# Score products interleaved with the second feed-forward product, and half of the query masks ahead of the activations

## The reference, cut to what matters

```python
def favor(x, omega):
    xs = x * dh ** (-0.25)
    u = jnp.einsum('bshd,dm->bshm', xs, omega)
    h = 0.5 * jnp.sum(xs * xs, axis=-1, keepdims=True)
    return jnp.concatenate([jnp.exp(u - h), jnp.exp(-u - h)], axis=-1) * m ** (-0.5)
# causal linear attention, per head: S += k v^T, z += k; out = (q S) / (q z + eps)
for l in range(3):
    q, k, v = (out @ W[l] + b[l] for each of q, k, v)        # in heads
    a = causal_linear_attention(favor(q), favor(k), v) @ Wo[l] + bo[l]
    h = layer_norm(out + a, ln1_g[l], ln1_b[l])
    y = jax.nn.relu(h @ W1[l] + bf1[l]) @ W2[l] + bf2[l]
    out = layer_norm(h + y, ln2_g[l], ln2_b[l])
```

## Time and profile before

| | |
|---|---|
| runs | 2047.53 us (2046.19 to 2049.01) |
| the profiled execution's own time | 2053.53 us |
| its span | 2051.6 us |
| busy in the span | PE 82%, DVE 76%, POOL 48%, ACT 43% |
| `attention()` | about 632 us to 1860 us of the span |
| in 655 to 1890 us | PE 1141.79 us busy of 1235, DVE 985.58, ACT 529.05, POOL 436.63 |

### The profile page before, as it was taken

The page is one execution under the profiler, slowest core; times in us unless marked ns, Lnnn a source line. Parts: engine busy times, 40 slices in busy tenths (PEclk is TensorE's granted clock), DMA queues, the critical chain, the costliest instruction groups (busy, mean ns, idle before and its releaser), DMA issues. The chain is left out here.

```text
span 2051.6 us, 69397 instructions
## 1 busy us (share of the span) xinstructions
PE 1680.2 (82%) x28443; PEld 1259.8 (61%) x28445; DVE 1554.3 (76%) x3835; ACT 883.3 (43%) x1642; POOL 983.6 (48%) x1045
## 2 busy tenths in 40 slices
PE   5655555469937999999999989999989999995798
PEld 4332334359935666766666766666766666663798
DVE  2899965359976878878888878888868878885675
ACT  2555555446623444444444434444434444442321
POOL 0677747769953224234234224224224224223797
PEclk7877765579977999999999999999999999997899
DMA  7400011122230000000000000000000000000001
GB/s 202 86 0 0 0 24 34 34 63 63 64 111 2 3 3 3 3 3 3 3 3 3 3 4 3 3 3 3 3 4 3 3 3 3 3 3 1 16 31 37
DMA packets 60732, 42.92 MB, mean 21 GB/s; under 512 B 19720, under 2 KB 54800, under 8 KB 59952
## 3 DMA queue, kind: packets, MB, share of 16 engines
q1 hardware_dynamic: 47504, 25.35, 4.7%
q0 software_dynamic: 4352, 8.99, 1.3%
q10 hardware_dynamic: 8608, 4.67, 0.9%
HBM read 24.22 MB, written 14.77 MB: 19 GB/s over the span
## 5 line engine op out<-in xcount | busy, mean ns | idle before, releaser
L368 POOL TENSOR_TENSOR at_rstd<-at_mv,const 128x4 f32<-128x4 f32 x96 | 19.5, 203 | 570.0 <-DVE at_mv L362 569.9
L1622 PE MATMUL psum<-attn_w,at_qa 128*128 128x128 f32 x1536 | 184.1, 278 | 0.0
L1614 PE MATMUL psum<-at_vT,attn_w 128*128 128x512 f32 x384 | 180.5, 613 | 1.4 <-ACT at_vT L1427 0.9
L1622 PEld LDWEIGHTS psum<-attn_w,at_qa 128*128 128x128 f32 x1536 | 175.2, 192 | 2.7 <-issue 0.6
L1431 ACT ACTIVATE at_qa<-psum,attn_bf 128x512 f32<-128x512 f32 x192 | 132.0, 687 | 90.2 <-PE psum L1614 90.2
L1326 DVE TENSOR_SCALAR at_kb<-at_kf,const 128x512 f32<-128x512 f32 x192 | 157.9, 882 | 0.0
L1332 DVE STREAM_TRANSPOSE at_vb<-at_vT 32x512 uint32<-32x512 uint32 x192 | 134.7, 702 | 1.9
L1848 PE MATMUL psum<-tilesT,ti_masked 128*128 128x128 f32 x1024 | 119.9, 279 | 12.9 <-POOL ti_masked L1810 12.9
L1848 PEld LDWEIGHTS psum<-tilesT,ti_masked 128*128 128x128 f32 x1024 | 117.8, 195 | 14.6 <-issue 14.6
L1556 PE MATMUL psum<-at_state,at_qa 64*64 64x36 f32 x3072 | 116.8, 242 | 9.6 <-issue 9.2
L1435 ACT ACTIVATE at_qa<-at_qf,const 128x512 f32<-128x512 f32 x192 | 122.3, 710 | 0.0
(11 more groups left out here) (303 smaller groups left out, 4315.2 us busy)
## 6 DMA issues: line engine op xcount, KB each, us to landing
ex_xs<-sorted_x SPq DMA_DIRECT2D x80, 65.0 KB
x<-in_L_attn_x ACTq DMA_DIRECT2D x8, 512.0 KB, 8.5
ex_feats<-token_y SPq DMA_DIRECT2D x4, 1024.0 KB, 8.1
out<-x SPq DMA_DIRECT2D x16, 256.0 KB, 2.3
expert_w<-in_L_ffn_w SPq DMA_DIRECT2D x1, 2048.0 KB, 9.5
attn_w<-in_L_attn_W SPq DMA_DIRECT2D x2, 768.0 KB
token_y<-ex_y,ex_place POOLq DMA_INDIRECT x72
sorted_x<-ex_spare SPq DMA_DIRECT2D x1, 1040.0 KB, 8.3
```

The costliest lines, as they stand in the source:

```text
L1614: mm(bank(f.s, c), k.w1[:, f.l, c * P:(c + 1) * P], hT[f.s][:], start=True, stop=True).then_inc(hid_ready, 1)
L1622: last = mm(bank(f.s, 1)[:, c * D:(c + 1) * D], hidden[f.s][:, t, c * P:(c + 1) * P], k.w2[:, f.l, t, :], start=(t == 0 and c == 0), stop= ...
```

## The change

TensorE does the second feed-forward product in two halves and puts the first half of the scores between them; the second half of the scores stands behind the second half of the product. VectorE takes `causal(0)` ahead of the residual of `f` and `causal(1)` directly behind the statistics, ahead of all normalising; the statistics of a new group's input move behind the scan of the state. ScalarE makes the first two query masks ahead of the four activations, and the other two behind them.

```diff
 VectorE
                         last.then_inc(vb_ready, 1)
-                        if then and f and f.l == L - 1:
-                            mod_statistics(then)
                         dve.wait_ge(begun, n + 1)
                         dve.wait_ge(sum_ready, n + 1)
...
                         nc.vector.tensor_tensor_scan(...).then_inc(state_ready, 1)
+                        if then and f and f.l == L - 1:
+                            mod_statistics(then)
+                    if a:
+                        causal(0)
                     if f:
                         dve.wait_ge(ff_ready, n + 1)
                         (residual L1351, statistics)
                     if a:
-                        causal(0)
+                        causal(1)
                     ends = f and f.l == L - 1
                     if ends and then:
                         mod_normalise(then)
                     if f and not ends:
                         dve.wait_ge(res_rstd, f.count * 2 + 2)
                         normalise(... xn[f.s]).then_inc(xn_ready, 1)
-                    if a:
-                        causal(1)
 ScalarE
+                    if a:
+                        act.wait_ge(qf_ready, n + 1)
+                        masked_queries(s, 0)
                     if f:
                         for t in range(FT):  (L1431)
                     if a:
-                        act.wait_ge(qf_ready, n + 1)
-                        for i in range(HQ):  (L1435)
-                        last.then_inc(qa_ready, 1)
+                        masked_queries(s, 1).then_inc(qa_ready, 1)
 TensorE
+                def feed_forward_out(f, half):
+                    for t in (2 * half, 2 * half + 1):
+                        pe.wait_ge(hid_taken, f.count * FT + (t + 1 if t != 0 else 2))
+                        for c in range(GC):
+                            last = mm(bank(f.s, 1)[:, c * D:(c + 1) * D], hidden[f.s][:, t, c * P:(c + 1) * P], k.w2[:, f.l, t, :], ...)
+                    if half:
+                        last.then_inc(ff_ready, 1)
...
                     if f:
-                        for t in range(FT):  (L1622)
-                        last.then_inc(ff_ready, 1)
+                        feed_forward_out(f, 0)
                     if a:
                         (waits for cols_scaled, sum_taken, kb_ready, qa_ready)
                         scores(s, n, 0)
+                    if f:
+                        feed_forward_out(f, 1)
+                    if a:
                         scores(s, n, 1)
```

More of the change, by code:

```diff
@@ L1344, in slot @@
                         nc.vector.tensor_tensor_scan(whole, resets[:].rearrange("p w j -> p (w j)"), whole, 0.0, ALU.mult, ALU.add).then_inc(state_ready, 1)
-                    if f:
-                        s, n = f.s, f.count
-                        dve.wait_ge(hres_ready, n + 1)
-                        dve.wait_ge(ff_ready, n + 1)
-                        st.done(nc.vector.tensor_tensor(flat(res[s][:]), bank(s, 1), flat(hres[s][:]), ALU.add))
-                        statistics(nc, lambda c: res[s][:, c, :], stats[s], mv[s]).then_inc(res_stats, 1)
+                        if then and f and f.l == L - 1:
+                            mod_statistics(then)
                     def causal(i):
@@ L1360, in slot @@
                         causal(0)
+                    if f:
+                        s, n = f.s, f.count
+                        dve.wait_ge(hres_ready, n + 1)
+                        dve.wait_ge(ff_ready, n + 1)
+                        st.done(nc.vector.tensor_tensor(flat(res[s][:]), bank(s, 1), flat(hres[s][:]), ALU.add))
+                        statistics(nc, lambda c: res[s][:, c, :], stats[s], mv[s]).then_inc(res_stats, 1)
+                    if a:
+                        causal(1)
                     ends = f and f.l == L - 1
@@ L1401, in _, with masked_queries @@
             def _(act):
+                def masked_queries(s, half):
+                    for i in (2 * half, 2 * half + 1):
+                        last = nc.scalar.activation(qa[s][:, :, i, :], qf[s][:].rearrange("p (j i) -> p j i", i=SUB), ACT.Copy,
+                                                    scale=cst(k, "mask_a")[:, i:i + 1])
+                    return last
                 def slot(a, f, then):
@@ L1432, in slot @@
                     if a:
-                        act.wait_ge(qf_ready, n + 1)
-                        for i in range(HQ):
-                            last = nc.scalar.activation(qa[s][:, :, i, :], qf[s][:].rearrange("p (j i) -> p j i", i=SUB), ACT.Copy,
-                                                        scale=cst(k, "mask_a")[:, i:i + 1])
-                        last.then_inc(qa_ready, 1)
+                        masked_queries(s, 1).then_inc(qa_ready, 1)
                         act.wait_ge(state_ready, n + 1)
@@ L1572, in output_weights @@
                         last.then_inc(wo_ready, 1)
+                def feed_forward_out(f, half):
+                    for t in (2 * half, 2 * half + 1):
+                        pe.wait_ge(hid_taken, f.count * FT + (t + 1 if t != 0 else 2))
+                        for c in range(GC):
+                            last = mm(bank(f.s, 1)[:, c * D:(c + 1) * D], hidden[f.s][:, t, c * P:(c + 1) * P], k.w2[:, f.l, t, :],
+                                      start=(t == 0 and c == 0), stop=(t == FT - 1), skip_group_check=True)
+                    if half:
+                        last.then_inc(ff_ready, 1)
                 def slot(a, f, then):
@@ L1618, in slot @@
                     if f:
-                        for t in range(FT):
-                            pe.wait_ge(hid_taken, f.count * FT + (t + 1 if t != 0 else 2))
-                            for c in range(GC):
-                                last = mm(bank(f.s, 1)[:, c * D:(c + 1) * D], hidden[f.s][:, t, c * P:(c + 1) * P], k.w2[:, f.l, t, :],
-                                          start=(t == 0 and c == 0), stop=(t == FT - 1), skip_group_check=True)
-                        last.then_inc(ff_ready, 1)
+                        feed_forward_out(f, 0)
                     if a:
```

## The result

| | before | after |
|---|---|---|
| median of 5 runs each, us | 2047.53 (2045.37 to 2053.09) | 2056.16 (2055.66 to 2057.95) |
| ratio after to before | | 1.004, 95% interval 1.0025 to 1.0054 |
| profiled execution's own time, span, us | 2053.53, 2051.6 | 2056.23, 2054.3 |

The changed kernel is slower, by 8.6 us, and 2054 us with a range of 2042 to 2066 was predicted. The two profiled executions stand only 2.7 us apart, since that of before is 6.0 us above its own median and that of after 0.1 us.

The account below looks back on a forecast made before the run. TensorE's list was taken to set the pace, busy 1141.79 of 1235 us. To the 2047.5 us median it added 5.5 us (46 slots at 0.12) and 1 for stalls left, 6.5 more: 2054 us, range 2042 to 2066.

Parts of the forecast that it names:

- The two chains: At the slot's tail, TensorE's order and VectorE's `at_xn` chain are nearly even; the change delays `at_xn`, TensorE waits 0.9 us.
- The slot within a group: Ordinary slot forecast at 25.22 us, 0.64 more than the slot read and 0.14 less than the mean.
- the price of splitting: TensorE's feed-forward product in halves: 0.21 us for tiling changes at both ends, bounds -0.05 and 0.4.
- The stalls: TensorE's unnamed waits in small matmuls, 26.1 us before L1563, read as instruction fetch; mostly gone, 1 us left.
- The start of a group: Slot starting a new group, second such slot and the one behind: 24.82, 26.22 and 26.16 us, with GpSimd late.
- The rival by which GpSimd's lateness doesn't reach the end: Behind a new group, GpSimd's lateness doesn't reach the slot's end: 25.09 us a slot, 2036 us; chance 0.12.
- Cost nothing: ScalarE's two early masks, 1.28 us, fit its 1.32 us wait for L1614; at most 0.1 us if L1431 starts late.
- The sum: Six slots take 152.9 us, 25.48 each against 25.36; 46 slots give 5.5 us, stalls left 1, together 6.5.
- The two loop jumps: TensorE at the loop's jumps: 6.3 us lost at each, 12.6 taken out for the mean slot.
- changes of tiling are free: Rival: TensorE's tiling changes cost nothing, L1622 ends 0.96 us later, slot within a group 25.01, total 2048 us; chance 0.2.
- the stalls stay: Rival: TensorE's unnamed waits remain, each slot takes 0.64 us more, 29 us in all, 2077 us; chance 0.08.

Follow-up runs that it names:

- e8: Changed kernel with `at_xn` announced and transposed in quarters into two banks, ScalarE scaling in two halves within a group; 2046.24 us, 1.0002 of before.
- e4: Changed kernel with the second weighed half ahead of the transposes of the next input; 2068.44 us, ratio 1.0127 to before.
- e6: Kernel before with only two query masks moved ahead of ScalarE's four activations, run again on another chip; 2038.32 us, ratio 0.9959 to before.
- e9: e6's kernel with TensorE's wait for the state moved ahead of the scores, in slots within a group; 2058.26 us, ratio 1.005 to before.
- e1: Kernel before with only two query masks moved ahead of ScalarE's four activations, first look; 2037.66 us, ratio 0.9972 to before.
- e7: The changed kernel unchanged, repeated on the chip of e5, e6 and e8; 2056.24 us, ratio 1.005 to before.
- e2: Changed kernel with all four query masks back behind ScalarE's activations; 2084.86 us, ratio 1.0204 to before.
- e5: Kernel before, built anew without change and run against itself; 2048.27 us, ratio 1.0002.

## Why the prediction was right, and where it was not

**The two chains.** Right, and shown. The transposes wait 0.82 us for `at_xn` where 0.9 was said, the wait stands in 45 slots, and e8, which shortens that chain by 0.54 us, makes the slots within a group 0.34 us shorter in the mean and 0.54 at best. L1359 starts 1367.89 - 1348.73 = 19.16 us into the slot, 19.05 was said.

**The slot within a group.** 25.31 against 25.22. The slot of the earlier trace rows from which it was counted isn't a clean one: it holds an unnamed wait of 0.28 us in the first weighed half, and the shortest slots of before take 24.33. This didn't reach the forecast, which goes through VectorE's chain. The 0.09 is in the price of splitting: both halves of L1583 and of L1552 take 1.99 + 1.09 + 1.98 + 0.98 = 6.04 us from start to start, where the earlier trace rows have 875.35 - 869.66 = 5.69. One more change to the 64x64 tiling and one back cost 0.35 us, and 0.21 was taken from bounds of -0.05 and 0.4. The halves of the product came as said, 1.99 each; what was left out is that the first half of the scores takes 1.09 and not 0.96. The Trainium skill (TensorEngine Tiling (Array Packing), Key Properties) says that changing the tiling mode drains TensorE, and gives no price. These rows fit it and give a price; that it is a drain they don't show.

**The stalls.** Right on after, with more to it than was said. The unnamed waits before scores, carried state and weighed values, 39.5 us in before, are 2.6 in after. But e4 and e8 show that the wait for `at_xn` hides a part of them, and that they return when it goes. The Trainium skill (Runtime: NRT & Kernel Launch, Instruction fetch mechanics) calls the crossing of a block mostly hidden. By number the trace of before agrees: the instruction queue moved 193 packets between the starts of the second and the last slot, against 57 unnamed waits at these three places. But these cost 39.5 us, and e6 and e9 show that they move with the waits ahead of them and that kernels with the same work differ by 0.9% with them (0.9959 and 1.005, each to before on its own chip).

**The start of a group.** The parts were off, their sum not. Predicted were 24.82, 26.22 and 26.16, together 77.20; measured 25.16, 26.02 and 26.03, together 77.21. In the first slot the step from the transposes to the next slot takes 1.77 us and not 1.53, with 0.35 us of waiting for ScalarE in it where other slots have 0.17, which I had not seen, and GpSimd's L368 came 6.24 us into the slot and not 6.51. Six slots take 3 x 25.31 + 77.21 = 153.1 us, 152.9 was said. The rival by which GpSimd's lateness doesn't reach the end (2036) is out: of the 2.34 us counted, (26.02 - 25.16) + (26.03 - 25.31) = 1.58 arrive, and it needed less than 0.7.

**"Cost nothing", on ScalarE's masks.** This is the step that fell short. In the changed order the masks cost nothing, as after's timeline shows (the second pair ends at 1362.66 + 1.32 = 1363.98, the first scores start at 1364.64). But they were never weighed in the old order. Alone, in the old order, the masks gain 5 to 9 us (e1, e6), and I had said in e1's expectation that nothing would change. The profile had no row that named it: I asked only whether the array waits for the masks, and by e6 and e9 what they held up is TensorE's taking up of instructions. On the chip of e6 and e7 the change is thus 9 us won by the masks and 18 lost by the rest, and I had only the sum of the two in view. The shares hold for this order of the steps alone: in the interleaved order the same masks are worth some 29 us (e2).

**The sum.** Predicted 5.5 + 1 on the median, 6.5; measured 8.6 in medians. The traces take it apart. From the second slot's start to the last's, after takes 1183.65 - 1179.23 = 4.4 us more. The two loop jumps, which I had carried over at 12.6 us, cost 10.8 in after: 3.49 + 2.20 us for the one at 1218.61 and 3.52 + 1.56 for the other. (In before the second stands still for 3.88 us and not 3.73, so both are 12.7.) Without the jumps the slots take 6.2 to 6.3 us more, 6.5 was said, and the mean slot is 25.50 us, 25.48 was said.

The rest is the execution on which the sum rests, 6.0 us above its median. In e5 the same kernel took 2049.03, 4.5 less: 2.3 of these lie in the 46 slots, and 1.9 behind the last slot's start, which lies 219.7 us before the end in that execution and 217.8 in e5 and in after. A comparison with such an execution makes the change look cheaper than it is, by 5.9 us here; the jumps and the stretch behind the last slot take back 1.8 and 1.9. That 6.5 came as near to 8.6 as it did is therefore in part luck; that the slots were forecast to 0.1 us is not.

One sum of the prediction doesn't come out: four fifths of 0.55, 0.08 and half of 0.05 are 0.545 for slower by more, not 0.56.

**The rival "changes of tiling are free" (2048)** is out by the 0.35 us: the second half of the product ends 18.98 us into the slot, 1.28 later than in the earlier trace rows, where 1.17 was said and the rival has 0.96. So is "the stalls stay" (2077), by the waits.

What stays open: how the 23.7 us of stalls that after lost against e6 divide into those that the large matmuls between really avoid and those that only fall into the wait for `at_xn`. e4 puts 16.9 us back, but it also makes one run of 128 small matmuls out of two.

## What to carry to other kernels

When an engine's idle time has no name and lies on a grid of instructions, look at what the instruction stream waits for, not only at what the array waits for: a semaphore that is met before the array comes may still be late. Breaking up a run of small instructions helps only if what is put between doesn't feed the chain that ends the stage; here half of the scores went ahead of the one product that the next slot's input hangs on, and the steadier slot is a longer one. Take the parts of a change apart before judging it: here a part thought free was a gain and the named part the loss, and a part's worth depended on what was already in place.

## What the runs showed of the hardware

- **Fetches follow waits.** In the slots quoted the block was asked for 1.0 to 1.3 us after the last semaphore ahead of the scores was met (masks at 16.47, fetch at 17.5 to 17.7; state product at 15.66, fetch at 16.7 to 16.9; scan at 16.83, fetch at 17.8 to 18.0), while the array reached the scores at 17.68 or 17.69 in all three.
- **Slots that end in a wait are steadier.** The 16 slots of the loop within a group, without those that hold a jump, took 25.31 or 25.32 us in after and 24.33 to 25.97 in before: a stall that falls into a wait does not show. In the times it is less clear: the 7 runs of e7 lie within 4.6 us and the 30 of before on the same chip within 19, but e8, with a few of the stalls back, has 6 in 12 runs, and e6, with most of them, 9 in 12.
- **A loop jump and the clock.** After the jump TensorE had stood still for 3.49 us, and the windows of after show its granted clock (the third column from the end) at 0.50, the 1.2 GHz level, for the first 3.5 us, against 1.00, 2.4 GHz, in an ordinary slot:

```profile
1218.60:1220.40 1.80, 1.79 (x2) 0.84 (x3) 0.18 (x1) 0.00 (x0) 0.00 (x0) 0.50 0.03 9
1220.40:1222.10 1.70, 1.70 (x3) 0.67 (x2) 0.00 (x0) 0.69 (x1) 0.00 (x0) 0.50 0.00 0
...
1374.00:1376.00 2.00, 1.95 (x6) 1.00 (x7) 1.33 (x4) 0.93 (x2) 1.17 (x1) 1.00 0.00 0
```

The pair of L1592 takes 2.07 us there and 1.12 in other slots, and 2.20 us are lost until L1598 at this jump, 1.56 at the other, 2.56 at each in before.
